# Fourier-bias attention stage: all head groups of all sequences in one run, query and key parts read back group by group

## The reference

```python
q, k, v = jnp.split(x @ Wqkv.T, 3, axis=-1)      # 16 heads of 8 features
logits = jnp.einsum('bhqd,bhkd->bhqk', q, k) * scale
logits = logits + _fourier_bias(alpha, beta, t)[None]
logits = jnp.where(causal[None, None], logits, -jnp.inf)
attn = jax.nn.softmax(logits, axis=-1)
out = jnp.einsum('bhqk,bhkd->bhqd', attn, v)
return out.transpose(0, 2, 1, 3).reshape(b, t, d) @ Wout.T
```

## Time and profile before

| | us |
|---|---|
| time, median of 3 runs | 6686.75 |
| lowest and highest of them | 6683.01, 6694.7 |
| the profiled execution | 6685.4 |
| its span, first to last instruction | 6683.6 |
| the attention stage in it, first transfer issue to last `y_all` write | 1294 to 2956 |
| one batch, from one issue of L678 to the next | 402.8 (1771.01 to 2173.76) |

### The profile page before, as it was taken

How to read it: one execution, slowest core, us unless ns; L and a number is a source line. 1 busy time by engine, 2 the same in 40 slices (tenths; PEclk the granted TensorE clock), 3 DMA queues, 4 the chain that set the end, 5 groups by cost and what they waited for, 6 DMA issues and landing times. The chain is left out here.

```text
span 6683.6 us, 148998 instructions
## 1 busy us (share of the span) xinstructions
PE 5256.6 (79%) x55030; PEld 3176.6 (48%) x55030; DVE 4233.4 (63%) x5698; ACT 2953.9 (44%) x4797; POOL 2630.1 (39%) x1392
## 2 busy tenths in 40 slices
PE   4735777348488584867999999999999999999996
PEld 3623444212122121214666666666666666666664
DVE  4353111324142332348999989898889888989995
ACT  0001222113123131325666666666666666666663
POOL 0000000000000000017777777677766766777773
PEclk8657889769788686889999999999999999999997
DMA  0000100130200102002111211211121112111111
GB/s 18 0 8 14 28 28 28 20 43 0 29 0 1 28 1 28 1 15 64 36 38 37 57 36 36 57 35 37 34 57 36 35 41 53 36 36 42 35 38 46
DMA packets 153483, 202.80 MB, mean 30 GB/s; under 512 B 40920, under 2 KB 79714, under 8 KB 151662
## 3 DMA queue, kind: packets, MB, share of 16 engines
q1 hardware_dynamic: 153360, 201.17, 13.2%
HBM read 63.67 MB, written 11.53 MB: 11 GB/s over the span
## 5 line engine op out<-in xcount | busy, mean ns | idle before, releaser
L99 POOL TENSOR_TENSOR ln_post_rstd<-ln_post_var,neg_half 128x8 f32<-128x8 f32 x16 | 26.8, 1672 | 2919.6 <-DVE ln_post_var L80 2919.6
L1704 POOL TENSOR_TENSOR d_rnorm<-d_sq_clip,neg_half 128x32 f32<-128x32 f32 x192 | 1048.4, 5461 | 62.6 <-DVE d_sq_clip L1536 61.9
L1694 POOL TENSOR_TENSOR d_qk_swap<-d_qk_raw,d_rot 128x512 f32<-128x512 f32 x768 | 961.0, 1284 | 17.9 <-ACT d_qk_raw L1379 14.0
L866 DVE TENSOR_REDUCE c_mx<-c_ps 128x1 f32<-128x512 f32 (+3 forms) x768 | 416.6, 556 | 775.7 <-PE c_ps L737 771.9
L834 ACT ACTIVATE c_pt<-c_ps 128x512 f32<-128x512 f32 (+1 forms) x640 | 354.3, 554 | 1117.6 <-PE c_ps L752 1115.7
L1153 PE MATMUL d_pair<-d_wqkv,d_xin 128*128 (+1 forms) x1536 | 753.4, 614 | 93.5 <-DVE d_probs L1557 40.6
L766 PE MATMUL c_ps<-c_pt,c_vg 128*32 128x512 f32 (+3 forms) x1536 | 628.3, 506 | 4.7 <-DVE c_ots L871 4.7
L1681 POOL TENSOR_TENSOR d_probs<-d_probs,d_prec 128x1024 f32<-128x1024 f32 x192 | 369.2, 1923 | 454.3 <-DVE d_prec L1568 454.3
L1165 PE MATMUL d_pair<-ident,d_qk_part 128*128 128x128 f32 x3072 | 424.4, 277 | 140.3 <-DVE d_qk_part L1547 137.7
L1165 PEld LDWEIGHTS d_pair<-ident,d_qk_part 128*128 128x128 f32 x3072 | 353.2, 141 | 321.1 <-issue 241.9
L1518 DVE TENSOR_TENSOR d_qk_part<-d_qk_raw,d_rot 128x1024 f32<-128x1024 f32 x384 | 471.4, 1228 | 48.9 <-issue 38.3
(11 more groups left out here) (248 smaller groups left out, 9676.4 us busy)
## 6 DMA issues: line engine op xcount, KB each, us to landing
d_band<-d_own_t SPq DMA_DIRECT2D x768, 64.0 KB, 2.0
d_band<-d_prev_t SPq DMA_DIRECT2D x576, 64.0 KB, 2.0
d_v_prev<-d_v SPq DMA_DIRECT2D x192, 128.0 KB, 2.3
b_w<-in_L_ffn_w SPq DMA_DIRECT2D x64, 256.0 KB, 3.3
d_band_prev<-d_prev_t SPq DMA_DIRECT2D x192, 64.0 KB, 2.0
d_wqkv<-in_L_ffn_Wqkv SPq DMA_DIRECT2D x6, 1536.0 KB, 8.8
c_kp<-c_k_scratch SPq DMA_DIRECT2D x30, 256.0 KB
c_qp<-c_q_scratch SPq DMA_DIRECT2D x24, 256.0 KB
```

Of the source, the lines that this page charges most:

```text
L866: eng.tensor_reduce(mx[:, hh, qt, k0 // 512:k0 // 512 + 1], ps[:, S1B[c % 2], 0:nk], AX.X, ALU.max).then_inc(mx_done, 1)
L1694: mm = eng.tensor_tensor(qk_swap[:, which, :, out:out + hd], qk_raw[:, which, :, src:src + hd], rot[:, bass.ds(par, 1), which, 1, bass.ds( ...
L1704: eng.tensor_tensor(rnorm[:, :], sq_clip[:, :], neg_half[:, 0:2 * HEADS], ALU.pow).then_inc(rn_ready, 1)
```

## The change

The groups of all batches become one run of 16 steps with both halves: group 3's live half goes with the maxima of group 0 of the next batch. The step with maxima only is left once, at the start, and the step without maxima once, at the end. For that the preparation of batch b+1 is put ahead of the groups of batch b, and the finish of b follows them. The scratch tensors in DRAM get a copy per batch, a tensor of their own takes the bias rows of the keys, and the values (`c_ve`) get two slots. The read back is cut by groups: after a group's second logits are done, twelve transfers of 8 partitions x 4 heads x 1024 tokens (64 KB) bring the same four heads of the next batch. At the stage's start the constants that the first products need are loaded first and waited for alone. The splitting of queries and keys into parts stays on ACT and DVE as it was.

```diff
-        def groups(eng, b, body):
-
-            NG = H // GROUP
-            body(None, b * NG - 1, True)
+        PLACED = 16 * 2 * PARTS
+
+        def batches(eng, prepare, body, finish):
+
+
+            prepare(0)
+            body(None, 0, -1, True)
+            with eng.Fori(0, BATCH - 1) as b:
+                prepare(b + 1)
+                with eng.Fori(0, NG) as g:
+                    body(g, b, b * NG + g, True)
+                finish(b)
             with eng.Fori(0, NG - 1) as g:
-                body(g, b * NG + g, True)
-            body(NG - 1, b * NG + NG - 1, False)
+                body(g, BATCH - 1, (BATCH - 1) * NG + g, True)
+            body(NG - 1, BATCH - 1, BATCH * NG - 1, False)
+            finish(BATCH - 1)
...
+                def place_parts(b, g):
+
+                    eng.wait_ge(placed, (b * NG + g) * PLACED + 16 * PARTS)
                     for r in range(PARTS):
...
+                            eng.dma_start(to[8 * r:8 * r + 8, bass.ds(g * GROUP, GROUP), :],
+                                          rows[:, bass.ds(g * GROUP, GROUP), :]).then_inc(placed, 16)
...
+                eng.sem_inc(passed, 1)
+                keep_parts(0)
+                eng.wait_ge(out_dram_done, 48)
+                for g in range(NG // 2):
+                    place_parts(0, g)
+                place_maxima(0, 0)
+                for g in range(NG // 2, NG):
+                    place_parts(0, g)
+                with eng.Fori(0, BATCH - 1) as b:
+                    keep_parts(b + 1)
+                    with eng.Fori(1, NG) as g:
+                        place_maxima(g, b * NG + g)
+                        eng.wait_ge(out_dram_done, b * 32 + 80)
+                        eng.sem_inc(passed, 1)
+                        eng.wait_ge(s2_ready, (b * NG + g) * N2)
+                        eng.sem_inc(passed, 1)
+                        place_parts(b + 1, g - 1)
+                    place_maxima(0, b * NG + NG)
+                    eng.wait_ge(s2_ready, (b * NG + NG) * N2)
+                    eng.sem_inc(passed, 1)
+                    place_parts(b + 1, NG - 1)
+                with eng.Fori(1, NG) as g:
+                    place_maxima(g, (BATCH - 1) * NG + g)
...
-                eng.wait_ge(c_in, 16 * CONSTS)
+                eng.wait_ge(first_in, 48)
...
-                    eng.wait_ge(placed, (b + 1) * (16 * 2 * PARTS) + 16 * PARTS)
...
+                    if maxima:
+                        eng.wait_ge(placed, (G + 2) * PLACED + 16 * PARTS)
+                        eng.sem_inc(passed, 1)
```

More of the change, by code:

```diff
@@ L691, in _ @@
-                eng.wait_ge(m_in, 16 * BATCH * (H // GROUP))
-            CONSTS = 7 + PARTS + 1
+                        for to, src, part in ((qp, q_dram, Q_PART[r]), (kp, k_dram, K_PART[r])):
+                            rows = src[bass.ds(b, 1), part, :, :].rearrange("l p t -> (l p) t").rearrange("(h d) t -> d h t", d=DH)
+                            eng.dma_start(to[8 * r:8 * r + 8, bass.ds(g * GROUP, GROUP), :],
+                                          rows[:, bass.ds(g * GROUP, GROUP), :]).then_inc(placed, 16)
@@ L716, in _ @@
                         mm.then_inc(qkv_done, 1)
+                    if not isinstance(b, int):
+                        eng.wait_ge(m_ready, b * NG - NG + 1)
                     for t in range(TB):
@@ L784, in _, with finish @@
+                def finish(b):
                     eng.wait_ge(on_ready, (b + 1) * 8)
@@ L793, in _ @@
                     eng.wait_ge(batch_done, b + 1)
+                batches(eng, prepare, body, finish)
             def flat(x):
@@ L804, in _, with prepare @@
                 eng.wait_ge(zeroed, 1)
-                with eng.Fori(0, BATCH) as b:
+                def prepare(b):
                     eng.wait_ge(turned, b + 1)
@@ L836, in _, with body @@
-                    groups(eng, b, body)
+                def body(g, b, G, maxima):
+                    if g is not None:
+                        eng.wait_ge(pv_done, G * N2)
+                        eng.activation(vg[:, :, :, 0:DH + 1].rearrange("p t h d -> p t h d"),
+                                       ve[:, bass.ds(b % 2, 1), :, bass.ds(g * GROUP, GROUP), :].rearrange("p l t h d -> p (l t) h d"), ACT.Copy).then_inc(vg_ready, 1)
+                        for c in range(N2):
+                            width = sum(s[2] for s in S2[c][2])
+                            eng.wait_ge(s2_ready, G * N2 + c + 1)
+                            if c >= 4:
+                                eng.wait_ge(pv_done, G * N2 + c - 3)
+                            eng.activation(pt[c % 4][:, 0:width], ps[:, S2B[c % 4], 0:width], ACT.Exp).then_inc(exp_done, 1)
@@ L849, in split, with prepare @@
                         eng.drain()
-                split(kparts, kf, 1)
-                eng.sem_inc(parts_ready, 1)
-                with eng.Fori(0, BATCH) as b:
+                def prepare(b):
                     rows = y_all[:, bass.ds(b * TB, TB), :]
+                    if not isinstance(b, int):
+                        eng.wait_ge(turned, b)
                     eng.tensor_copy(xin[:], rows).then_inc(xin_ready, 1)
+                    if isinstance(b, int):
+                        split(kparts, kf, 1)
+                        eng.sem_inc(parts_ready, 1)
                     split(qparts, qf, 2 * b + 2)
@@ L898, in _, with finish @@
+                def finish(b):
+                    rows = y_all[:, bass.ds(b * TB, TB), :]
                     eng.wait_ge(out_done, b + 1)
```

239 lines of the change are left out of this document (117 added, 122 removed).

## The result

| | before | after |
|---|---|---|
| median of the runs, us | 6684.88 (6681.73 to 6694.7) | 6367.97 (6364.76 to 6375.15) |
| ratio, 95% interval | | 0.9527, 0.9513 to 0.9541 |
| span of the profiled execution, us | 6683.6 | 6373.4 |
| stage's first transfer issue | 1294.36 | 1298.26 |
| first product of maxima, from the stage's start | 138.2 | 80.3 |

The forecast was 6370 us, in a range from 6345 to 6410. The stage itself gave 57.8 + 260.4 = 318.2 us; this one trace is 3.9 us later ahead of the stage and 4.1 us behind it, where both kernels run the same instructions.

The account below looks back on a forecast made before the run. PE sets the pace in full steps; its four waits for read-back parts, 291.3 us, are the large non-computing item. Steps and passages gain 265.0, the start 52.0: 317.0 off 6685.4 gives 6368.4, forecast 6370 us, range 6345 to 6410.

Parts of the forecast that it names:

- Reads behind the work: A group's twelve reads, 14.5 us, hide under a 73 us step; slowing of PE bounded by 0 and 174, taken as 0.
- One passage: Between two batches: finish 5.5, VectorE's jump 3.2, splits 18.6, less 0.9, so 26.4 us after SP's maxima issue, twice.
- The first preparation: Behind the maxima-only step, without a finish: 18.6 us plus 1.9 for the way into the loop, 20.5 us.
- The step behind a preparation: Step after a preparation: maxima already landed and PE two chunks ahead save 5.0 us, three times; bounds 0 and 8.6.
- The third passage: Finish without preparation, ahead of the last full steps' end: taken as 3 us, bounds 1.1 to 6.5.
- The start: Way to the first product of maxima: early constants and one group's reads gain 52.0 us, bounds 10 and 57.
- Fixed costs and jumps: Some 2 us per transfer could make a group's reads 38 us, start gain 30; jumps counted 3.2 in two passages.
- A: Rival: small reads cost as much as large, 58 us a group, 95 us less gain, 6465 us; chance 0.04.
- B: Rival: reads disturb the steps' matmuls; in full 174 us lost, 6544 (chance 0.02); a third, 6428 (small form, 0.09).
- C: Rival: TensorE's low clock for whole steps, 52 us more each, 7150 us, slower than before; chance 0.02.
- D: Rival: better overlap (8.6 instead of 5.0), free jumps, start gaining 57: 22 us more gain, 6348 us; chance 0.08.
- E: Rival: some wait holds a read until the step needing it, 14.5 us per step, 218 in all, 6588; chance 0.02.

## Why the prediction was right, point by point

*What bounds the kernel.* Right. The one large item in the list of waits held 207.0 us for the three later batches, and 189.1 of them were won by removing the reads alone (kernel before without reads); the splits on VectorE took the rest.

*Reads behind the work.* Right, and the bound of 174 us for disturbed products can be struck: none, simple and double reads give 928.6, 929.4 to 929.9 and 931.4 us for the twelve intervals beside reads. The sum's zero was argued from no row; it is now shown. That the cover is a step's length fits the doubled reads, which stay under it, and the sixfold ones, which don't.

*One passage.* 26.4 us forecast, 1720.99 to 1747.37 = 26.4 measured, but by two errors that cancel. The finish takes 8.2 us (1719.83 to 1728.08), not 5.5: the granted clock was 1.00 from 1743 to 1749 us in the trace before and is 0.50 from 1720 to 1728 now. For the same 16 products that is 3.78 us (L843, above) against this row of before:

```profile
1745.89 2.05 PE L790 MATMUL c_ps<-c_w_out,c_ont 128*128 128x128 f32 x16 [1.11 <-ACT c_ont L838]
```

And VectorE's jump back shows as 0.7 us, not 3.2. The first could be seen in the trace before: the end of each step with both halves has a low stretch there that begins 3 to 7 us ahead of SP's issue of the maxima and ends 7 to 10 us behind it, and the finish now stands in such a place. The second is read from this trace; why it is shorter is not shown (see the jumps below). So the exact 26.4 is luck.

*The first preparation.* 20.5 + 73.3 - 5.0 = 88.8 forecast, 88.7 and 88.3 measured.

*The step behind a preparation.* 5.0 us less than a step was forecast; 1816.71 - 1747.37 = 69.3, so 4.0.

*The third passage.* 3 us forecast between 1.1 and 6.5; 78.6 - 73.3 = 5.3. This is the largest miss of a single interval. PE waits 2.00 us at the finish's end, until 2360.09, and again passes through a slow L843 (3.78 us at 2354.31, clock 0.50).

*The step.* 73.3 forecast, 73.4 in the mean of eleven.

*The sum.* 1160.8 forecast, 1165.4 measured; gain 260.4 instead of 265.0. The 4.6 us that are missing here and the 5.8 us that the start gave beyond its forecast nearly cancel, so that the total of 317.0 lies closer to the stage's 318.2 than its parts do.

*The start.* Gain 52.0 forecast, 57.8 measured, just above the upper bound of 57, and not for that bound's reason: the bias rows' write did wait behind the constants. The last term was too large: 13.2 us for a group, not 16, less than the 14.5 by size even without the 1.5 for the landing; the six full reads took 28.0, not 28.8; and from the stage's start the bias rows were in DRAM after 33.4 us, where 35.6 were forecast.

*Fixed costs and jumps.* Twelve quarter reads issued one behind the other on SP took 13.2 us, 1.1 each. By the Trainium skill ("DMA: Bandwidth & Descriptors", "Anatomy of one DMA — SWDGE (gpsimd) path") each transfer has a fixed cost of some 2 us, measured there on another issue path. Paid twelve times in a row it would make a group take 38 us by the prediction's estimate (and leave 28 us of the start's gain, not the 30 given there); for transfers queued like these the trace contradicts that with its 13.2 us. On the jumps, VectorE's jump back over batches shows as 3.1 to 3.3 us in all six cases of the kernel before and its version without reads, and as 0.7 us in every trace of the changed kernel and its variants. The code that is jumped over became shorter: with the repeated step counted once, a batch has 272 records of VectorE in the trace before and 152 after. The Trainium skill ("Runtime: NRT & Kernel Launch", "Instruction fetch mechanics") says that a taken branch whose target lies outside the pages held must fetch it first; the rows would fit that, and no run here varied the length alone.

*The rivals.* A (small reads cost as much as large) is out by the 13.2 us. B is out by the two kernels on reads. C (low clock in whole steps) is out: 0.89 to 0.93 in the table by stretches. D (more gain) came in at the start and in the jumps (2.5 us in each of two passages), but the slower finish took the latter back. Of the prediction's signs of being wrong, a wait for the maxima above 4.7 us did appear, 4.8 us once, in the last step, where no reads run, so it doesn't speak for A. E (a wait holds a read) did not occur: no wait of PE for parts behind the first group is longer than 2.0 us.

## What to carry to other kernels

A wait that recurs once per batch can be sized by its own row, and removing it gives that row's time less what the next limit holds: here 69 us a batch in the list, 63 won, because the splits on VectorE end later than the rest of the preparation. Cut a read by the unit that its consumer needs first, and ask of the rest whether it fits under one step; here 25 us of reads a group fitted and 86 us did not, and what broke were two places, the issuing engine and the queue. When one engine has to do something serial between two loops, look which engine stands idle there: GpSimd took 3.17 us for a pair of operations that VectorE does in 1.92, and the move still gave back 4 us per passage.

## What the runs showed of the hardware

- Twelve reads of 64 KB to 8 partitions, issued back to back on one queue: 13.2 us; of 256 KB: 57.9 us. For these two sizes the time goes by the bytes.
- Matmuls and vector reductions beside transfers at a DMA share of 0.17: PE busy 64.6 to 64.8 us of a step and VectorE 29.2 to 30.0, against 64.3 to 65.4 and 29.4 to 29.8 at a share of 0.00.
- GpSimd takes 2.13 us for a subtraction of 128x1024 fp32 and 1.04 us for the cast to bf16, VectorE 1.23 and 0.69 for the same.
- Eight filling products at a step's end cut the time at 1.2 GHz from 13.5 to 5.5 us per step and gave 1.3 us back. The clock falls before the long rest in one kernel and before the fillers in the other; these runs don't show what makes it fall.
- VectorE's jump back over batches cost 3.1 to 3.3 us in the long loop (six cases) and 0.7 us in the short one; only these two loops stand for it.
